# A Mamba phase with its second gate tile activated straight from PSUM, and other places for four kinds of work

## The reference, cut to what matters

```python
xz = x @ W_in.T
x_ssm, z = jnp.split(xz, 2, axis=-1)              # 512 channels each
xc = conv(x_ssm, conv_w) + conv_b                 # 4 taps along the sequence
x_ssm = silu(xc)
proj = x_ssm @ W_x.T                              # B (16), C (16), step (1)
dt = softplus(proj[..., -1:] * W_dt[:, 0] + b_dt)
# scan over t: h = exp(dt*A) * h + (x*dt) * B ;  y = sum_n h * C     (16 states)
y = (ys + x_ssm * D_param) * silu(z)
return y @ W_out.T
x = layernorm(x + attn(x))
# then, for the cross attention: q = x @ Wq, k = ctx @ Wk, v = ctx @ Wv
```

## Time and profile before

| | |
|---|---|
| median of three runs | 1657.34 us |
| the profiled execution's own time | 1650.65 us |
| its span | 1648.7 us |
| mean granted TensorE clock | 0.928 |
| VectorE (DVE) busy | 1408.0 us, 85% |
| TensorE (PE) busy | 1316.0 us, 80% |
| ScalarE (ACT) busy | 1123.0 us, 68% |
| GpSimd (POOL) busy | 1024.4 us, 62% |

### The profile page before, as it was taken

The page is one execution under the profiler, slowest core; times in us unless marked ns, Lnnn a source line. Parts: engine busy times, 40 slices in busy tenths (PEclk is TensorE's granted clock), DMA queues, the critical chain, the costliest instruction groups (busy, mean ns, idle before and its releaser), DMA issues. The chain is left out here.

```text
span 1648.7 us, 22427 instructions
## 1 busy us (share of the span) xinstructions
PE 1316.0 (80%) x7436; PEld 920.8 (56%) x7436; DVE 1408.0 (85%) x2530; ACT 1123.0 (68%) x2548; POOL 1024.4 (62%) x711
## 2 busy tenths in 40 slices
PE   6788788777887787788777879889988998897870
PEld 4566566656666666666555644456445644462460
DVE  5899999999999999999997856597869786978678
ACT  5877888888789878988886523348534853475570
POOL 2799899999999999999988511003700370027025
PEclk9988999999999998999997979999999999999995
DMA  6101210221022102211210023000010000000000
GB/s 206 68 1 68 81 63 20 81 81 62 21 82 81 53 30 81 81 34 48 75 70 31 20 105 118 1 1 1 26 56 1 0 26 26 1 1 1 26 1 25
DMA packets 44581, 76.40 MB, mean 46 GB/s; under 512 B 3825, under 2 KB 38226, under 8 KB 40242
## 3 DMA queue, kind: packets, MB, share of 16 engines
q1 hardware_dynamic: 44466, 74.98, 13.1%
HBM read 66.06 MB, written 8.91 MB: 45 GB/s over the span
## 5 line engine op out<-in xcount | busy, mean ns | idle before, releaser
L974 POOL TENSOR_TENSOR state_c<-state,c_area 128x1024 f32<-128x1024 f32 x256 | 600.7, 2362 | 28.7 <-DVE state L1051 23.6
L1051 DVE TENSOR_TENSOR_SCAN state<-decay,ps 128x512 f32<-128x512 f32 x416 | 503.6, 1213 | 15.6 <-ACT decay L729 14.2
L729 ACT ACTIVATE decay<-step_area,negA 128x255 f32<-128x255 f32 x832 | 351.6, 497 | 0.5 <-DVE step_area L1129 0.5
L1662 POOL TENSOR_TENSOR big<-big,g_sb 128x1024 f32<-128x1024 f32 x29 | 79.4, 2739 | 404.4 <-ACT big L1551 402.7
L1019 DVE TENSOR_TENSOR ps<-step_area,ps 128x512 f32<-128x512 f32 x416 | 283.6, 682 | 16.9 <-PE ps L410 14.6
L426 PE MATMUL ps<-ident_sb,state_c 128*128 128x128 f32 x2048 | 288.7, 290 | 0.7 <-POOL state_c L974 0.7
L426 PEld LDWEIGHTS ps<-ident_sb,state_c 128*128 128x128 f32 x2048 | 257.0, 151 | 25.7 <-issue 12.9
L943 POOL TENSOR_TENSOR ub<-step_area,b_bc 128x1024 f32<-128x1024 f32 x48 | 113.5, 2364 | 27.9 <-DVE step_area L1132 27.9
L1510 PE MATMUL ps<-w_sb,hT 128*128 128x256 f32 x512 | 120.3, 389 | 2.5 <-ACT hT L1620 1.9
L1051 DVE TENSOR_TENSOR_SCAN state<-ps,ub 128x512 f32<-128x512 f32 x96 | 116.1, 1209 | 6.6 <-ACT ps L742 6.1
L1475 PE MATMUL ps<-w_sb,weights 128*128 128x512 f32 x256 | 121.0, 608 | 0.0
(11 more groups left out here) (214 smaller groups left out, 2476.5 us busy)
## 6 DMA issues: line engine op xcount, KB each, us to landing
c_area<-bc_scratch SPq DMA_DIRECT2D x32, 1024.0 KB, 7.9
b_bc<-bc_scratch SPq DMA_DIRECT2D x16, 384.0 KB, 4.6
weights<-in_xT SPq DMA_DIRECT2D x16, 256.0 KB, 3.2
res<-in_x SPq DMA_DIRECT2D x16, 256.0 KB, 2.8
x_scratch<-res SPq DMA_DIRECT2D x16, 256.0 KB, 2.1
weights<-x_scratch SPq DMA_DIRECT2D x4, 1024.0 KB, 9.0
xa<-x_scratch SPq DMA_DIRECT2D x4, 1024.0 KB, 5.7
out_x<-acc SPq DMA_DIRECT2D x4, 1024.0 KB, 4.8
```

The source lines that it names most:

```text
L729: nc.scalar.activation(decay_tile(i, n)[:, j, 1:], dt_sb[:, i[1] % 2, j, 1:], ACT.Exp, scale=negA[:, j * NS + n:j * NS + n + 1]).then_inc( ...
L974: nc.gpsimd.tensor_tensor(state_c[:, n % RING, :, :], state[:, n % RING, :, :], c_bc[:, q, n, :].unsqueeze(1).to_broadcast([P, CT, TC]), A ...
L1051: nc.vector.tensor_tensor_scan(state[:, n % RING, pair, :].rearrange("p j n -> p (j n)"), a, b, 0.0, ALU.mult, ALU.add).then_inc(s_scan, 1)
```

## The change

ScalarE's copy of the second z tile is gone: the tile stays in `w_ps` until `silus`, which writes its Silu straight into `gate`. The first z tile is still copied (slot 8) and goes through a Silu of its own, last of the three. The wait for `s_y` (that the gate buffer is free) moves ahead of the new Silu. `s_zc` counts the copy and the new Silu, so `project` on PE now waits for the new Silu. `normalise` goes from the list's slot 13 to the end of slot 15, after `first_decay` (in turn 15 before `spare_keys`). In turn 15 PE's `context` 0 to 3 go from slots 1, 2, 2, 3 to 1, 2, 3, 4, `values` from 3, 4 to 5, 6, `query` 0 to 4 from 5, 6, 7, 8, 9 to 7, 7, 8, 9, 10; ScalarE's `take_context` from 5, 6, 6, 7 to 5, 5, 6, 7, `take_values` from 7, 8 to 8, 9, `take_query` from 9 to 13 to 10, 10, 11, 12, 13. `y_back`, `out_tile`, `query` 5 and 6 keep their slots.

```diff
-        zc = y_sb
+        zc = y_sb[:, 0, :]
...
                 if i[1] == NCH - 1:
-                    work += [(0, lambda: keys(1)), (1, lambda: context(0)), (2, lambda: context(1)), (2, lambda: context(2)),
-                             (3, lambda: context(3)), (3, lambda: values(False)), (4, lambda: values(True))]
-                    work += [(5 + v, lambda v=v: query(v)) for v in range(G + 1)]
+                    work += [(0, lambda: keys(1)), (1, lambda: context(0)), (2, lambda: context(1)), (3, lambda: context(2)),
+                             (4, lambda: context(3)), (5, lambda: values(False)), (6, lambda: values(True))]
+                    work += [(7 + max(v - 1, 0), lambda v=v: query(v)) for v in range(G + 1)]
...
-            def take_z(k, t):
-                act.wait_ge(s_in, at(k, 4, 2 + t + 1))
-                nc.scalar.activation(zc[:, t, :], w_ps[:, :], ACT.Copy).then_inc(s_zc, 1)
+            def take_z(k):
+                act.wait_ge(s_in, at(k, 4, 3))
+                nc.scalar.activation(zc[:, :], w_ps[:, :], ACT.Copy).then_inc(s_zc, 1)
...
                 nc.scalar.activation(xs[:, q, :, :], xs[:, q, :, :], ACT.Silu).then_inc(s_silu, 1)
-                act.wait_ge(s_zc, at(k, CTT, CTT))
+                act.wait_ge(s_in, at(k, 4, 2 + CTT))
+                act.wait_ge(s_y, at(k, 16, 16))
+                nc.scalar.activation(gate[:, q, 1, :], w_ps[:, :], ACT.Silu).then_inc(s_zc, 1)
                 if k[1] == 1:
                     nc.scalar.activation(gate[:, 0, :, :], gate[:, 0, :, :], ACT.Silu).then_inc(s_gate, 1)
-                act.wait_ge(s_y, at(k, 16, 16))
-                nc.scalar.activation(gate[:, q, :, :], zc[:, :, :], ACT.Silu).then_inc(s_gate, 1)
+                act.wait_ge(s_zc, at(k, CTT, 1))
+                nc.scalar.activation(gate[:, q, 0, :], zc[:, :], ACT.Silu).then_inc(s_gate, 1)
...
                 if settle:
-                    work += [(0, lambda: take_sum(old, 0)), (1, lambda: take_sum(old, 1)), (5, lambda: spreads(old)), (8, lambda: guess(old)),
-                             (13, lambda: normalise(old))]
+                    work += [(0, lambda: take_sum(old, 0)), (1, lambda: take_sum(old, 1)), (5, lambda: spreads(old)), (8, lambda: guess(old))]
                 if prepare:
-                             (8, lambda: take_z(k, 0)),
-                             (9, lambda: take_z(k, 1)), (10, lambda: silus(k)), (11, lambda: copies(k)),
+                             (8, lambda: take_z(k)),
+                             (10, lambda: silus(k)), (11, lambda: copies(k)),
...
                 if prepare:
                     work.append((15, lambda: first_decay(k)))
+                if settle:
+                    work.append((15, lambda: normalise(old)))
                 if i[1] == NCH - 1:
-                    work += [(4, lambda: take_keys(1)), (5, lambda: take_context(0)), (6, lambda: take_context(1)),
-                             (6, lambda: take_context(2)), (7, lambda: take_context(3)), (7, lambda: take_values(False)),
-                             (8, lambda: take_values(True))]
-                    work += [(9 + v, lambda v=v: take_query(v)) for v in range(G + 1)]
+                    work += [(4, lambda: take_keys(1)), (5, lambda: take_context(0)), (5, lambda: take_context(1)),
+                             (6, lambda: take_context(2)), (7, lambda: take_context(3)), (8, lambda: take_values(False)),
+                             (9, lambda: take_values(True))]
+                    work += [(10 + max(v - 1, 0), lambda v=v: take_query(v)) for v in range(G + 1)]
```

More of the change, by code:

```diff
@@ L792, in turn @@
                 if settle:
-                    work += [(0, lambda: take_sum(old, 0)), (1, lambda: take_sum(old, 1)), (5, lambda: spreads(old)), (8, lambda: guess(old)),
-                             (13, lambda: normalise(old))]
+                    work += [(0, lambda: take_sum(old, 0)), (1, lambda: take_sum(old, 1)), (5, lambda: spreads(old)), (8, lambda: guess(old))]
                 if prepare:
-                    work += [(3, lambda: take_xi(k, 0)), (4, lambda: take_xi(k, 1)), (5, lambda: take_conv(k, 0)), (7, lambda: take_conv(k, 1)), (8, lambda: take_z(k, 0)),
-                             (9, lambda: take_z(k, 1)), (10, lambda: silus(k)), (11, lambda: copies(k)),
+                    work += [(3, lambda: take_xi(k, 0)), (4, lambda: take_xi(k, 1)), (5, lambda: take_conv(k, 0)), (7, lambda: take_conv(k, 1)), (8, lambda: take_z(k)),
+                             (10, lambda: silus(k)), (11, lambda: copies(k)),
                              (12, lambda: terms(k, 0)), (12, lambda: terms(k, 1)), (12, lambda: terms(k, 2)),
```

## The result

| | before | after |
|---|---|---|
| median of five runs | 1657.34 us (1655.27 to 1659.65) | 1641.34 us (1639.43 to 1648.39) |
| ratio | | 0.9914, 95% interval 0.9888 to 0.9940 |
| the profiled execution's own time | 1650.65 us | 1639.43 us |
| ratio when run again beside the experiments (17 runs of before, 6 of after) | | 0.9934 (0.9921 to 0.9947) |

Faster, as forecast. The sizes differ a little by what is asked: the two medians are 16.0 us apart, the first ratio makes 14.2 us of 1657.34, the repeated one 10.9, the two profiled executions 11.2. The forecast was 9.1. Five runs of the changed kernel span 9 us, so a few microseconds of a median mean little here; the traces say more, and there the place of the 11.2 us can be read.

A forecast was written before the change was run, and what follows sets the result against it. VectorE was taken to set the pace, so only its idle time could be won: 5.6 us from the turns plus 3.5 from the last turn, 9.1 off the 1657.34 us median, gives 1648.2 us; range 1643 to 1653.8.

The forecast's parts named there:

- What bounds it: State-space phase: VectorE sets the pace, busy 58.5 of 60 us; only its idle time can be won.
- Part 1: z tiles on ScalarE: chain to slot 13's decay 0.38 us shorter per turn, 5.6 us over 15 waits.
- Part 2: Normalisation moved from slot 13 to after slot 15: worth 0; stage load lands 4.3 us later, not waited for.
- Part 3: Last turn: new PE slots make VectorE 5.9 us earlier, 3.5 us kept because PE's own queue ends the phase.
- Last turn gives nothing: Rival, chance 0.15: the queries' bunching at slot 7 gives back all of the last turn's gain; 1651.7 us.
- no gain per turn: Rival, chance 0.1: PSUM Silu takes its 1.04 bound, or y_back becomes the thing before decay 13; 1653.8 us.
- Last turn gives all: Rival, chance 0.15: out_tiles and queries keep up, so the last turn gives 7 us; 1644.7 us.
- Slower: Rival, chance 0.05: TensorE's clock stays low in the last turn's slots 5 to 10; 1664 us.
- The rule that was weighed against it: Last turn: transposes don't count as activity raising TensorE's clock, so PE would enter values and queries at 1.2 GHz.

The follow-up runs named there:

- z_alone: Kernel before with only the z-tile part: second z tile through Silu straight from PSUM, normalise and last turn as before; ratio 0.9968 to before.
- query_apart: Changed kernel with turn 15's queries 0 to 4 at PE slots 7, 8, 9, 10, 10, not 7, 7, 8, 9, 10; ratio 0.9933 to before.
- last_alone: Kernel before with only turn 15's contexts, values and queries at their new slots; ratio 0.9967 to before.
- queries_later: Changed kernel with queries 5 and 6 moved behind round_max(0) and (1), query 7 behind round_max(2); ratio 0.9931 to before.
- chain_shorter: Changed kernel without ScalarE's Copy of the first z tile from the chunk of turn 1 on, that computation left out; ratio 0.9901 to before.
- y_back_late: Changed kernel with ScalarE's two take_y_back at slots 13 and 14 of a prepared turn instead of 12 and 13; ratio 0.9886 to before.

## Why the prediction was right or wrong

**What bounds it** was right: VectorE's busy time is unchanged, its idle time paid for everything, and in five kernels each change of ScalarE's chain is found again in the turn, to 0.01 us (table).

**Part 1.** The durations were right (0.58 and 0.62 us for 0.60 and 0.61; the chain 0.43 for 0.38), and so was the wait that is left (0.82 for 0.85). By time, z_alone gives 5.3 us (interval 2.8 to 7.6) for the forecast 5.6. That the sum of the decay waits fell by just 5.6 in the first trace is luck: the second has 10.7, 3.5 less than before. In the first trace the b_row waits and two waits for `state_c` grew while others shrank, 1.4 us of it back in all, but as such waits differ as much between executions of one order, that they come from the change is not shown. One turn was counted wrongly: in turn 14 ScalarE waits for PE's `y_back` ahead of the `decay` of 13 (1.69 us before, 2.10 after), so what is cut before that wait is not gained there; the prediction had this as a rival for all turns. That `project` starts where it did held to 0.1 us: it began 0.14 us after the end of the Silu of z at 560.63, 8.75 us after the first z Copy, where it had been 8.66. The b_row behind it is still waited for in some turns, as before.

**Part 2.** Forecast 0: right for the kernel as it is, with 0.5 us in the last turn that was not foreseen. Alone it showed 2.7 us the other way, not explained. The load of `stage` was issued 10.74 us before `context(0)` (862.13 to 872.87) where it had been 13.36, 2.6 us later and not the 4.3 of the working: the store ahead of it took 2.1 us to free SP, where it had taken 3.9. It landed in 5.7 us, and nothing waited for it.

```profile
859.56 0.37 SPq L284 DMA_DIRECT2D x_scratch<-res  x1
861.70 0.38 SPq L248 DMA_DIRECT2D res<-in_x  x1
862.13 0.47 SPq L279 DMA_DIRECT2D weights<-x_scratch  x1
```

**Part 3.** The mechanism was right in its order: no wait before the b_row of 6, none worth counting before 9, one of 3.41 (forecast 3.8) before 10, and PE's own queue at the end (query_apart). The mis-sized term is the length of that queue. It was put at 26.9 us from the b_row of 10 to `round_max(0)`; it took 25.3 (899.25 to 924.58). The slots that the working prices are nearly right: the three with a query were put at 2.9 us and take 2.77, 0.4 less in all, the two with an output tile at 3.6 and take 3.94 and 3.15. The other 1.1 us lie in the rest (the `y_back`s, queries 5 and 6 and the last states), put at 11.0 without an account of its parts and measured at 9.9. The b_row of 10 itself came 0.6 us nearer to `take_y` (23.28 for 23.9), and that was there already at the b_row of 7: `context(3)` was put at 1.1 us, its duration at TensorE's lower level, and took 0.66. Together that is the 2.2 us between the forecast 3.5 and the measured 5.65, and nearly all of the miss of the sum: 9.1 forecast, 11.2 between the two profiled executions.

**The rivals.** *Last turn gives nothing* and *no gain per turn* fall by last_alone and z_alone. *Last turn gives all* (7 us) is what the outcome leans to, but queries_later and query_apart show that the part kept is set by PE. *Slower* fell with TensorE's clock: it was granted 0.83 of full speed from 870 to 880, 1.00 from 880 on, where before it had stood at 0.50 from 880 to 890.

```profile
870.00:880.00 10.00, 5.83 (x36) 5.08 (x34) 9.47 (x14) 7.76 (x24) 9.92 (x8) 0.83 0.00 0
880.00:890.00 10.00, 8.28 (x47) 5.03 (x48) 9.96 (x15) 6.42 (x21) 9.76 (x8) 1.00 0.01 2
```

The rule that was weighed against it (the Trainium skill, "TensorE: Matmul & The Clock Gate", Part 4: PE-mode transpose) is not borne out here either. What PE ran between 872.87 and 878.18, while the same four transposes went from 1.09 to 0.60 us, was transposes, but for one b_row of 0.42 us.

## What to carry to other kernels

A wait that comes once a turn and ends on a long unbroken row of work of another engine can be priced from that row: here 0.40 to 0.51 us in the row, at its start, in its middle or near its end, were the same in the turn. Measure it by the length of turns that have no other wait, not by the sum of one kind of wait: an earlier wait for another engine can stand in for the one at the end (the b_row's), and a second wait on the same row can take part of the gain (the PSUM decay's in chain_shorter). Look first for an instruction that need not stand before the awaited one at all: y_back_late moves one in a single line, for as much per turn (0.48) as the rebuilt z work gives (0.43). Where side work shares one bank with a strict order, put the emptying of the bank ahead of anything on that engine that waits, and ask which engine's queue ends the phase before smoothing the other one's waits.

## What was not expected of the hardware

The state-space turns of one and the same instruction order took 854.6 us in one execution (26.39 to 881.00) and 861.0 in another (27.05 to 888.04). The lists of waits differ in VectorE's waits for b_row (4.7 against 9.2 us), for the PSUM decays (6.1 against 7.4) and for `take_y` (0.6 against 2.4). TensorE's `project` took from 1.97 to 3.51 us in one trace by the level of its clock, and the b_row stands right behind it. That TensorE's clock makes the spread of the runs is not shown: its mean over a run says little of the run's time. Of 29 runs of the kernel before, the fastest (1648.86 us) has 0.926, the slowest (1661.37) 0.928, and two with 0.933 took 1653.86 and 1657.57. No run was made to tell more.
